# Finished rows of the experts scattered back to their tokens, the last layer's into the output

## The chip, the cores and the metric

The program runs on one core of a Trainium2 chip. The core has TensorE (PE, matmuls), VectorE (DVE), ScalarE (ACT), GpSimd (POOL) and SyncE (SP), and 16 DMA engines. The metric is the device time of one execution in microseconds; lower is better.

## The reference

Six sub-layers over 4 x 512 = 2048 tokens of 128 numbers: a ternary-weight feed-forward, a softmax attention with a second "moving" term, the same feed-forward, then a routed feed-forward, a linear attention, and the routed feed-forward again. The routed one is what the change is about:

```python
    def _L1_ffn_ref(x, Wr, W1, W2):                      # x is the normalised input
        probs = softmax(xf @ Wr); eidx = argmax(probs)   # E = 8 experts
        rank = number of earlier tokens with the same expert
        keep = rank < cap                                # cap = 2048 / 8 = 256
        xe = xf[dispatch]                                # [E, cap, 128]
        h = jnp.maximum(jnp.einsum('ecd,edf->ecf', xe, W1), 0.0)
        ye = jnp.einsum('ecf,efd->ecd', h, W2) * (pe * valid)[:, :, None]
        y = zeros.at[dispatch].add(ye)                   # dropped tokens get 0
    x = x + 0.5 * _L1_ffn_ref(_layernorm(x), ...)
    x = x + _L1_attn_ref(_layernorm(x), ...)
    x = x + 0.5 * _L1_ffn_ref(_layernorm(x), ...)
```

With the given inputs one or two experts get nearly all tokens: 556 tokens are kept in the first routed layer and 572 in the second; the other slots of the 8 x 256 stay empty.

## The kernel before

The order of every engine's work is written out by hand; engines wait on semaphores. The tokens stand in SBUF as four batches `x[b]`, each 128 partitions x 4 tiles x 128. A batch is normalised (DVE's `moments` and `normalise`, with the root between them on POOL, `rsqrt`), turned by TensorE, and so on.

A routed layer goes so. For each batch DVE works out (`place`, L1009) for each token a row number `slot_all` and a factor `gate_all` (0 for a dropped token); a dropped token has a spare row behind the 2048 real ones. POOL sends the four tiles of normalised rows to these rows of `xe_scr` in HBM (`scatter`, L569, four indirect DMAs of 128 rows). When all are there, SP loads each expert's 256 rows (`rows_in`, L494), and for each of eight experts TensorE turns them (L1677), multiplies by the first weights (`up`), ACT and DVE apply the relu to one half each (L870, L1214), TensorE multiplies by the second weights (`down`), DVE copies the result from PSUM (L1218), SP stores it to `ye_scr` (L500). TensorE does `up` of the next expert ahead of `down` of this one; results, hidden tiles and rows have 2, 2 and 4 buffers.

Then the answers come back by token. After the first routed layer POOL gathers for each batch four tiles of 128 rows of `ye_scr` by `slot_all` (`gather`, L577 to L587), and DVE's `combine` (L1220) adds gate times row to `x[b]` and goes on with the norm of the linear attention. The gathers of batches 1 to 3 stand in POOL's row between its other work of that attention. After the second routed layer POOL gathers all sixteen tiles (L720), DVE sums (L1371), SP stores `x[b]` to the output (L538).

The rows that a dropped token points to in `ye_scr`, and the rows of `xe_scr` that no token fills, are set to zero by four DMAs at the start (L344); DVE waits for them ahead of its fourth batch.

## Time and profile before

| | us |
|---|---|
| three runs | 706.55, 710.32, 709.92 (median 709.92) |
| the profiled execution | 705.89 |
| its span, first to last instruction | 704.1 |
| busy: PE / DVE / ACT / POOL | 506.5 / 365.7 / 196.7 / 181.9 |
| mean granted TensorE clock | 0.881 of full speed |

The first routed layer's expert stage lies at 415 to 453 us of the span, the linear attention's entries at 462 to 500, its loop to 622, the second expert stage at 639 to 676, the rest is the way back to the output. A chain of waits follows the work that ended last back through what released it; a timeline lists the instructions of an engine with the idle time ahead of each and what ended it.

### The profile page before, as it was taken

The numbers are of one execution on the slowest core, as the hardware profiler recorded it, in microseconds if no ns is written. First come the engines' busy times: TensorE is split into PE (matmuls) and PEld (weight loads), VectorE is DVE, ScalarE is ACT, GpSimd is POOL, SyncE is SP. The second block draws the span as 40 slices with busy tenths as digits, with TensorE's granted clock in tenths as the row PEclk, the third lists the DMA queues.
The fourth block names the chain that finished last, engine by engine and source line by source line (L and its number), as shares of the span: only waits on it lengthen the run. The fifth ranks groups of instructions, "written<-read, shape, count | busy, mean of one in ns | idle before, by whom it ended". The sixth has DMA issues, their size and how long they took to land.

```text
span 704.1 us, 9924 instructions
## 1 busy us (share of the span) xinstructions
PE 506.5 (72%) x3706; PEld 323.5 (46%) x3706; DVE 365.7 (52%) x950; ACT 196.7 (28%) x278; POOL 181.9 (26%) x208
## 2 busy tenths in 40 slices
PE   1777775998899999988686639634788888735930
PEld 1654322445444544533475528522454655424920
DVE  4555482668667676820655412135778777330221
ACT  1454313451543245065235002112123111101200
POOL 8564360000101010010023350044402022031035
PEclk9999896999999999999999559956999999656975
DMA  7537877332633422060430021107652620001213
GB/s 267 210 117 244 266 246 197 120 99 62 139 101 89 126 80 80 29 159 15 134 106 16 19 64 49 38 27 178 186 149 54 190 70 16 1 16 52 61 41 101
DMA packets 61471, 74.16 MB, mean 105 GB/s; under 512 B 6772, under 2 KB 38128, under 8 KB 61168
## 3 DMA queue, kind: packets, MB, share of 16 engines
q1 hardware_dynamic: 59376, 69.34, 33.6%
q0 software_dynamic: 2048, 4.20, 2.1%
q8 instruction: 29, 0.48, 0.3%
q14 instruction: 18, 0.15, 0.1%
HBM read 42.97 MB, written 30.41 MB: 104 GB/s over the span
## 4 chain that ended last, share of the span: by engine, by line
PE 46%; DVE 17%; POOL 8%; SPq 8%; issue 8%; DMA 7%; ACT 5%; POOLq 0%; DVEq 0%; ACTq 0%
PE ps_accum L1379 21%; PE ps_pair L1379 15%; PE ps_turn L1379 5%; POOL xe_scr L574 3%; DMA sb_ring<-sb_qs 3%; SPq L358 2%; DVE sb_work L1133 2%; PE ps_turn L1387 2%; POOL sb_work L720 2%; POOL sb_rstd L558 2%; DVE sb_work L1271 2%; DVE sb_mpart L1059 1%; SPq L352 1%; DVE sb_stats L960 1%; DVE sb_values L969 1%
## 5 line engine op out<-in xcount | busy, mean ns | idle before, releaser
L812 ACT ACTIVATE sb_work<-ps_pair 128x1024 f32<-128x1024 f32 x80 | 80.3, 1026 | 50.7 <-PE ps_pair L1379 49.8
L1379 PE MATMUL ps_pair<-sb_ring,sb_xsets 128*128 128x512 f32 x160 | 64.6, 480 | 11.4 <-DMA sb_ring<-sb_qs 5.7
L1059 DVE TENSOR_REDUCE sb_mpart<-ps_turn 128x4 f32<-128x512 f32 x80 | 55.0, 687 | 31.2 <-PE ps_turn L1379 31.1
L1059 DVE TENSOR_REDUCE sb_mpart<-ps_accum 128x4 f32<-128x512 f32 x80 | 55.0, 688 | 19.2 <-PE ps_accum L1379 18.2
L1379 PE MATMUL ps_accum<-sb_work,sb_v_aug 128*32 128x128 f32 (+3 forms) x768 | 57.7, 394 | 0.3 <-ACT sb_work L812 0.3
L1379 PE MATMUL ps_turn<-sb_ring,sb_m_sets 128*128 128x512 f32 x80 | 39.5, 494 | 10.0 <-DVE sb_mpart L1059 9.8
L1379 PE MATMUL ps_accum<-sb_ring,sb_m_sets 128*128 128x512 f32 x80 | 41.8, 523 | 4.5 <-DVE sb_mpart L1059 3.9
L1379 PEld LDWEIGHTS ps_pair<-sb_ring,sb_xsets 128*128 128x128 f32 x160 | 30.7, 199 | 22.5 <-issue 10.7
L624 POOL TENSOR_TENSOR sb_e_pad<-sb_v_next,sb_y_ar 128x128 f32<-128x128 f32 x16 | 7.3, 457 | 127.2 <-DVE sb_y_ar L1103 127.2
L1271 DVE TENSOR_TENSOR sb_work<-ps_pair,sb_cst 128x1024 f32<-128x1024 f32 x32 | 37.5, 1214 | 2.2 <-PE ps_pair L1379 2.2
L1133 DVE TENSOR_TENSOR sb_work<-ps_pair,sb_cst 128x1024 f32<-128x1024 f32 x32 | 37.7, 1218 | 0.9
L556 POOL TENSOR_SCALAR sb_ve<-sb_mv 128x4 f32<-128x4 f32 x24 | 5.6, 233 | 124.5 <-DVE sb_mv L963 124.3
L1379 PE MATMUL ps_pair<-sb_y_tmp,sb_mw 128*128 128x256 f32 x128 | 34.1, 414 | 1.9 <-ACT sb_y_tmp L862 1.9
L574 POOL DMA_INDIRECT xe_scr<-sb_values,sb_slot_all x16 | 15.9, 994 | 73.4 <-DVE sb_slot_all L1040 69.8
L1387 PE MATMUL ps_turn<-sb_cst,sb_values 128*128 128x128 f32 x48 | 10.3, 354 | 34.1 <-DVE sb_values L969 29.6
L1379 PE MATMUL ps_accum<-sb_mw,sb_work 128*128 128x128 f32 x256 | 31.3, 276 | 2.3 <-issue 2.3
L1379 PE MATMUL ps_pair<-sb_xs,sb_w1r 128*128 128x512 f32 x64 | 22.1, 470 | 15.0 <-DVE sb_xs L979 7.4
L1379 PEld LDWEIGHTS ps_accum<-sb_mw,sb_work 128*128 128x128 f32 x256 | 30.0, 192 | 2.8 <-issue 2.6
L1218 DVE COPY sb_e_pad<-ps_accum 128x256 f32<-128x256 f32 x16 | 6.8, 425 | 44.7 <-PE ps_accum L1379 44.7
L1379 PE MATMUL ps_pair<-sb_ring,sb_ka_stk 128*128 128x512 f32 x64 | 24.4, 492 | 7.6 <-DVE sb_work L1271 4.9
L734 ACT COPY sb_xnT<-ps_turn 128x512 f32<-128x512 f32 x16 | 9.3, 583 | 70.6 <-PE ps_turn L1387 70.6
L1379 PEld LDWEIGHTS ps_pair<-sb_y_tmp,sb_mw 128*128 128x128 f32 x128 | 25.4, 210 | 6.6 <-ACT sb_y_tmp L862 3.4
(242 smaller groups left out, 1002.2 us busy)
## 6 DMA issues: line engine op xcount, KB each, us to landing
sb_m_sets<-q_scr SPq DMA_DIRECT2D x16, 256.0 KB
sb_xsets<-k_scr SPq DMA_DIRECT2D x16, 256.0 KB
sb_ka_stk<-mk_scr SPq DMA_DIRECT2D x4, 1024.0 KB
sb_mw<-in_mw SPq DMA_DIRECT2D x16, 256.0 KB, 5.6
sb_ka_stk<-mk_scr SPq DMA_DIRECT2D x8, 512.0 KB
q_scr<-sb_qs SPq DMA_DIRECT2D x12, 256.0 KB, 3.1
k_scr<-sb_ks SPq DMA_DIRECT2D x12, 256.0 KB, 3.9
sb_ring<-k_scr SPq DMA_DIRECT2D x64, 48.0 KB
```

Source lines behind the costliest of these rows:

```text
L358: sp.dma_start(ring[VW * hl:VW * hl + 3 * HD, i, hl].bitcast(F32), head_rows(q_scr, b, HL * hs + hl, 3 * HD)).then_inc(done, 16)
L558: pool.tensor_tensor(rstd[i][:], ve[i][:], const("minus_half"), ALU.pow).then_inc(s["rstd"], 1)
L574: pool.indirect_dma_start(xe_scr, bass.IndirectOffsetOnAxis(ap=places[:, t:t + 1], axis=0), rows_out[:, t, :], None).then_inc(s["scattered ...
L624: pool.tensor_tensor(dst, value, answer, ALU.subtract).then_inc(s["err_pad"], 1)
L720: pool.indirect_dma_start(y_last[:, b, t, :], None, ye_scr, bass.IndirectOffsetOnAxis(ap=slot_all[:, i:i + 1], axis=0)).then_inc(last_gath ...
L734: act.copy(dst, bank[:]).then_inc(s["x2_ready"], 1)
L812: act.activation(banks[:, 2 * i:2 * i + 2], pair[u % 2][:], ACT.Exp, scale=SCALE).then_inc(s["exp_done"], 1)
L1059: dve.tensor_reduce(mpart[:, m // NPAIR, m % NPAIR, :], max_banks[m % 2][:].rearrange("p (h k) -> p h k", h=HL), AX.X, ALU.max).then_inc(s ...
L1133: dve.tensor_tensor(work[:, n % 4].rearrange("p a (h q) -> p (a h) q", h=HL), pair[n % 2][:].rearrange("p a (h q) -> p (a h) q", h=HL), bc ...
L1271: dve.tensor_tensor(work[:, n % 4].rearrange("p a (h q) -> p (a h) q", h=HL), pair[n % 2][:].rearrange("p a (h q) -> p (a h) q", h=HL), bc ...
L1379: return pe.matmul(dst, lhsT, rhs, start=start, stop=stop, skip_group_check=True)
L1387: last = pe.transpose(tile(dst, t), src[:, t, :], ident)
```

## The change

1. A row that goes out to the experts (`rows_out`) has 258 numbers: the 128 normalised ones, the token's number, its gate, and the 128 of the not normalised x (`RW = 2 * D + 2`; `ID, GATE, OLD = D, D + 1, D + 2`). DVE writes them at once in this layout; there is one more small DVE instruction in `place`. The two layers have an `xe_scr` each.
2. On evacuation DVE does 2 multiply-adds instead of a copy: result x gate + old x. So what leaves an expert is the finished row of its token.
3. POOL casts the row numbers of the loaded rows (`places_of`) and scatters each expert's two tiles straight to `y_scr` (first layer) or `out` (second) while the next experts run. Before, SP has stored every batch's old x there (`keep_old`), for the dropped tokens.
4. An empty slot carries a number from 2048 on. In the first layer these rows go behind the real ones of `y_scr`; for `out` the DMA has a bound on the row number, and skips them. To this end SP fills the first 2048 rows of each `xe_scr` (six DMAs of 128-column or 2-column runs) ahead of the experts' weights.
5. After the first layer SP loads `x[b]` from `y_scr`; `combine` is now `entry`, without the sums. After the second nothing is left but SP's wait. All gathers, the fills at the start, `gate_all` and the four stores of `x[b]` go.
6. The rows out of the first layer lie where `ring` is, so POOL sets that part to zero again ahead of `scatter_back(0)`; SP waits for it ahead of the linear attention's first stores. The experts' rows and the second layer's rows out share the place of `e_pad`.
7. A load of rows into one of the four buffers now waits for the evacuation of the expert that had it, too.

```diff
-            def gather(b): ...
+            def places_of(n):
+                pool.wait_ge(xg_loaded[n % 4], 16 * (n // 4 + 1))
+                if n >= 4:
+                    pool.wait_ge(ye_kept[n % 2], 16 * NG * ((n - 2) // 2))
+                pool.tensor_copy(places_back[:, n % 4, :], xg[:, n % 4, :, ID]).then_inc(s["places_in"], 1)
+            def scatter_back(m):
+                for kept in old_kept[m]:
+                    hold(pool, kept, 16 * B // (m + 1))
+                places_of(E * m)
+                for e in range(E):
+                    n = E * m + e
+                    if e + 1 < E:
+                        places_of(n + 1)
+                    pool.wait_ge(s["places_in"], n + 1)
+                    hold(pool, s["ye_evac"], n + 1)
+                    for g in range(NG):
+                        pool.indirect_dma_start(y_scr[m], bass.IndirectOffsetOnAxis(ap=places_back[:, n % 4, g:g + 1], axis=0),
+                                                ye[n % 2][:, g, :], None, bounds_check=(2 - m) * NTOK - 1,
+                                                oob_is_err=False).then_inc(ye_kept[n % 2], 16)
...
+            pool.wait_ge(s["scattered"], 16 * NT * B)
+            pool.wait_ge(old_kept[0][0], 16 * B)
+            pool.memset(ring[:, 0:2].bitcast(F32), 0.0).then_inc(s["zeroed"], 1)
+            pool.memset(ring[:, 2, 0, 0:B * NT * RW - 2 * HL * T].bitcast(F32), 0.0).then_inc(s["zeroed"], 1)
+            scatter_back(0)
...
+                dve.tensor_scalar(rows_out[r // B][b][:, :, ID], spare[:], float(-NTOK), None, ALU.add)
...
-                    dve.tensor_copy(ye[:, n % 2].rearrange("p g d -> p (g d)"), accum[n % 2][:, 0:NG * D]).then_inc(s["ye_evac"], 1)
+                    for g in range(NG):
+                        last = dve.scalar_tensor_tensor(out=ye[n % 2][:, g, :], in0=accum[n % 2][:, g * D:(g + 1) * D],
+                                                        scalar=xg[:, n % 4, g, GATE:GATE + 1], in1=xg[:, n % 4, g, OLD:RW],
+                                                        op0=ALU.mult, op1=ALU.add)
+                    last.then_inc(s["ye_evac"], 1)
...
+            for scr in xe_scr:
+                spill = scr[0:NTOK].rearrange("(p r) d -> p r d", p=P)
+                for c, src in ((0, bc(const("ident"), NTOK // P)), (OLD, bc(const("ident"), NTOK // P)),
+                               (ID, const("spill_ids").rearrange("p (r d) -> p r d", d=2))):
+                    sp.dma_start(spill[:, :, c:c + src.shape[2]], src).then_inc(s["spill_in"], 16)
...
+            for b in range(B):
+                sp.dma_start(x[b][:], tile_rows(y_scr[0], b)).then_inc(x_loaded[b], 16)
+            hold(sp, s["zeroed"], 18)
```

POOL's row from the last scatter of the second layer to its end, before (`sb_work` is where the answers by token landed):

```order
L558 TENSOR_TENSOR sb_rstd<-sb_ve,sb_cst 128x4 [waits s_var_eps]
L574 DMA xe_scr<-sb_values,sb_slot_all 4096x128 [waits s_rank_j,s_pad_zero]
L574 DMA xe_scr<-sb_values,sb_slot_all 4096x128 x3
L720 DMA sb_work<-ye_scr,sb_slot_all 128x128 [waits s_ye_mm,s_ye_kept1,s_ye_kept0]
L720 DMA sb_work<-ye_scr,sb_slot_all 128x128 x15
```

and of the change (`sb_expert_rows` the loaded rows, `sb_y_tmp` the finished ones, `sb_places_back` their row numbers):

```order
L566 TENSOR_TENSOR sb_rstd<-sb_ve,sb_cst 128x4 [waits s_var_eps]
L585 DMA xe_scr<-sb_exit_rows,sb_slot_all 4096x258 [waits s_rank_j]
L585 DMA xe_scr<-sb_exit_rows,sb_slot_all 4096x258 x3
L593 CAST sb_places_back<-sb_expert_rows 128x2 [waits s_kept1,s_kept2,s_ye_kept0,s_xg0]
L593 CAST sb_places_back<-sb_expert_rows 128x2 [waits s_ye_kept1,s_xg1]
L607 DMA out<-sb_y_tmp,sb_places_back 2048x128 [waits s_places_in,s_ye_evac]
L607 DMA out<-sb_y_tmp,sb_places_back 2048x128
L593 CAST sb_places_back<-sb_expert_rows 128x2 [waits s_ye_kept0,s_xg2]
...
L607 DMA out<-sb_y_tmp,sb_places_back 2048x128 [waits s_places_in,s_ye_evac]
L607 DMA out<-sb_y_tmp,sb_places_back 2048x128
```

The sixteen gathers behind the last evacuation are gone, and sixteen scatters stand in pairs, each behind its expert's evacuation (`s_ye_evac`). The same pairs stand in the first layer.

SP's row ahead of and behind the first expert stage, before (`sb_mw` the experts' weights):

```order
L400 DMA sb_ring<-sb_qs 1x4x512
L477 DMA sb_mw<-in_mw 128x512 [waits s_st_mm,s_ma_mm]
L478 DMA sb_mw<-in_mw 128x4x128
...
L494 DMA sb_e_pad<-xe_scr 128x2x128 [waits s_scattered]
L494 DMA sb_e_pad<-xe_scr 128x2x128 x3
L494 DMA sb_e_pad<-xe_scr 128x2x128 [waits s_xg_t]
L500 DMA ye_scr<-sb_e_pad 128x2x128 [waits s_ye_evac]
...
L500 DMA ye_scr<-sb_e_pad 128x2x128 [waits s_ye_evac] x5
L352 DMA mq_scr<-sb_qs 16x8x512 [waits s_l1_lo]
```

and of the change:

```order
L397 DMA sb_ring<-sb_qs 1x4x512
L476 DMA xe_scr<-sb_cst 2048x1x128 [waits s_st_mm]
L476 DMA xe_scr<-sb_cst 2048x1x128
L476 DMA xe_scr<-sb_cst 2048x1x2
...
L479 DMA sb_mw<-in_mw 128x512 [waits s_ma_mm]
...
L483 DMA y_scr<-sb_wide_rows 128x4x128 [waits s_ffn_x] x4
L504 DMA sb_expert_rows<-xe_scr 128x2x258 [waits s_scattered,s_kept0,s_spill_in]
L504 DMA sb_expert_rows<-xe_scr 128x2x258 x3
L504 DMA sb_expert_rows<-xe_scr 128x2x258 [waits s_ye_evac,s_places_in,s_xg_t] x4
L511 DMA sb_x<-y_scr 128x4x128 [waits s_ye_kept0,s_ye_kept1]
...
L349 DMA mq_scr<-sb_qs 16x8x512 [waits s_zeroed,s_l1_lo]
```

The fills stand ahead of the weights, the old x is stored ahead of the first rows' load, the stores of the answers are gone, and the four loads of x wait for both of POOL's semaphores.

## Rows read from the trace of the kernel before

**Rows 1.** The page: span, and the chain that ended last by line.

```profile
span 704.1 us, 9924 instructions
...
PE ps_accum L1379 21%; PE ps_pair L1379 15%; PE ps_turn L1379 5%; POOL xe_scr L574 3%; DMA sb_ring<-sb_qs 3%; SPq L358 2%; DVE sb_work L1133 2%; PE ps_turn L1387 2%; POOL sb_work L720 2%; POOL sb_rstd L558 2%; DVE sb_work L1271 2%; DVE sb_mpart L1059 1%; SPq L352 1%; DVE sb_stats L960 1%; DVE sb_values L969 1%
```

**Rows 2.** Chain of waits, 640 us to the end: start, us, what.

```profile
675.82 0.44 DVE sb_e_pad L1218
...
678.10 0.73 issue
...
697.62 2.36 DMA sb_work<-ye_scr,sb_slot_all
```

**Rows 3.** Chain of waits from 450 to 470 us.

```profile
452.60 0.44 DVE sb_e_pad L1218
...
463.17 0.89 DVE sb_stats L960 x4
```

**Rows 4.** Timeline 655 to 675 us: start, us, engine, line, operation, count, [idle before <-releaser].

```profile
658.26 0.68 DVE L1214 TENSOR_SCALAR sb_work<-ps_pair 128x512 f32<-128x512 f32 x1
...
659.67 1.95 PE L1379 MATMUL ps_accum<-sb_mw,sb_work 128*128 128x128 f32 x16
...
661.65 0.42 DVE L1218 COPY sb_e_pad<-ps_accum 128x256 f32<-128x256 f32 x1 [2.71 <-PE ps_accum L1379]
662.00 0.68 DVE L1214 TENSOR_SCALAR sb_work<-ps_pair 128x512 f32<-128x512 f32 x1
...
666.92 0.38 PE L1677 MATMUL ps_turn<-sb_cst,sb_e_pad 128*128 128x128 f32 x2
...
673.76 1.47 PE L1379 MATMUL ps_accum<-sb_mw,sb_work 128*128 128x128 f32 x11 [1.16 <-issue]
```

**Rows 5.** Timeline of POOL; last, the sixteen last gathers: ns min/median/max.

```profile
413.70 1.82 POOL L676 MEMSET sb_h_act<- 128x2048 f32 x1
...
588.07 1.09 POOL L574 DMA_INDIRECT xe_scr<-sb_values,sb_slot_all  x1 [20.55 <-DVE sb_slot_all L1040]
589.46 0.97 POOL L574 DMA_INDIRECT xe_scr<-sb_values,sb_slot_all  x1 [0.31 <-issue]
...
L720 POOL DMA_INDIRECT sb_work<-ye_scr,sb_slot_all x16: 940/944/999, 678.8 to 697.6; - x16
```

**Rows 6.** Chain of waits, start of the first expert stage.

```profile
412.56 2.22 DMA xe_scr<-sb_v_next,sb_slot_all
414.80 2.23 DMA sb_e_pad<-xe_scr
```

**Rows 7.** Timelines of SP and of DVE at the start.

```profile
0.73 0.45 SPq L318 DMA_DIRECT2D sb_x<-in_x  x1
...
3.65 0.87 DVE L960 BATCH_NORM_STATS2 sb_stats<-sb_x 128x6 f32<-128x128 f32 x4 [3.65 <-DMA sb_x<-in_x]
```

**Rows 8.** Timelines of DVE and TensorE, entries of the second attention.

```profile
466.17 1.32 DVE L969 TENSOR_SCALAR sb_values<-sb_x,sb_mv,sb_rstd 128x128 f32<-128x128 f32 x4 [1.60 <-POOL sb_rstd L558]
...
493.66 1.21 PE L1379 MATMUL ps_pair<-sb_ring,sb_ka_stk 128*128 128x512 f32 x4 [2.31 <-DMA sb_ka_stk<-mk_scr]
...
494.92 2.34 DVE L1271 TENSOR_TENSOR sb_work<-ps_pair,sb_cst 128x1024 f32<-128x1024 f32 x2
...
502.50 1.10 DVE L969 TENSOR_SCALAR sb_values<-sb_x,sb_mv,sb_rstd 128x128 f32<-128x128 f32 x4
...
526.63 1.13 DVE L1224 SCALAR_TENSOR_TENSOR sb_x<-sb_e_pad,sb_gate_all,sb_x 128x128 f32<-128x128 f32 x4
```

**Rows 9.** Timelines of SP and POOL; then stretches: us, TensorE busy, clock, DMA share, GB/s.

```profile
343.01 0.35 SPq L477 DMA_DIRECT2D sb_mw<-in_mw  x1
...
378.15 1.25 POOL L574 DMA_INDIRECT xe_scr<-sb_y_tmp,sb_slot_all  x1 [6.89 <-DVE sb_slot_all L1040]
...
416.00:420.00 4.00, 2.32 (x6) 0.50 0.53 159
608.00:644.00 36.00, 14.00 (x78) 0.50 0.11 33
```

More of the change, by code:

```diff
@@ L255, in build @@
         v_scr = dram("v_scr", [B, T, D])
-        xe_scr = dram("xe_scr", [2 * NTOK, D])
-        ye_scr = dram("ye_scr", [2 * NTOK, D])
+        xe_scr = [dram(f"xe_scr{m}", [2 * NTOK, RW]) for m in range(2)]
+        y_scr = [dram("y_scr", [2 * NTOK, D]), out]
         def tile_rows(ap, b):
@@ L534, in _ @@
                     load_l1(b + 1, 1)
-            experts(1)
-            for b in range(B):
-                sp.wait_ge(s["mixed"], NT * (B + b + 1))
-                sp.dma_start(tile_rows(out, b), x[b][:]).then_inc(s["out_done"], 16)
-            sp.wait_ge(s["out_done"], 16 * B)
-            for kept in ye_kept:
-                sp.wait_ge(kept, 16 * E)
-            sp.wait_ge(s["scattered"], 16 * NT * B * 2)
+                if b:
+                    hold(sp, s["l1_x"], b)
+                    keep_old(1, b - 1)
+            hold(sp, s["l1_x"], B)
+            keep_old(1, B - 1)
+            experts(1)
         @block.gpsimd
@@ L693, in _ @@
             rsqrt(norm_of_entry(1), 1)
-            gather(2)
             base(1)
@@ L950, in _ @@
             router_exp(2 * B - 1)
-            act.wait_ge(s["scattered"], 16 * NT * 2 * B)
+            for left in sent[1]:
+                act.wait_ge(left, 16 * NT * B // 2)
             relu_experts(1)
@@ L1676, in turn_rows @@
                     for g in range(NG):
-                        last = pe.transpose(tile(turn[n % 2], g), xg[:, n % 4, g, :], ident)
+                        last = pe.transpose(tile(turn[n % 2], g), xg[:, n % 4, g, 0:D], ident)
                     last.then_inc(s["xg_t"], 1)
```

166 lines of the change are left out of this document (74 added, 92 removed).

## The prediction

> **What bounds the kernel now.** I read the page first. The chain that ended last runs through TensorE's matmuls into its three kinds of PSUM tiles for 41% of the span (21, 15 and 5), so what matters is which handovers stand between its busy stretches [rows 1]. So I read the chain in order of time next, at the two places that the change touches: from the first expert stage into the second attention, and from the second expert stage to the end.
>
> At the end nothing but POOL works. The last expert result leaves PSUM at 675.82 + 0.44 = 676.26; then come the store of the answers, 0.73 us before POOL's first gather, sixteen gathers one behind the other of which the last starts at 697.62, its landing and the sum behind it [rows 2]. From 676.26 to the span's end at 704.1 that is 27.84 us. At the first stage's end it is the same pattern for one batch: last result at 452.60 + 0.44 = 453.04, DVE's statistics of batch 0 start at 463.17, so 10.13 us [rows 3].
>
> Inside an expert stage TensorE sets the pace: DVE's relu of one expert starts 662.00 - 658.26 = 3.74 us after that of the expert before, and TensorE starts on the relu's tile at 659.67, 0.73 us after the relu ended (658.26 + 0.68). Only the last expert is different: there TensorE waits 1.16 us for a relu that stands behind an evacuation [rows 4].
>
> **End of the second stage.** The sixteen gathers, the sixteen sums and the four stores of the output go. In their place POOL scatters each expert's two tiles when they are evacuated. Only the last expert's pair lies behind the end of TensorE's work. From evacuation to landing: 0.02 to wake, 0.75 before the first DMA (0.73 at 678.10), 1.39 from its start to the second's (588.07 to 589.46, first 1.09 and 0.30 of issue) [rows 2, 5], and 2.22 from a scatter's start to its landing [rows 6]: 4.38 us, say 4.5 with SP's last wait. 27.84 - 4.5 = 23.3 us gained.
>
> This holds if POOL keeps up. Per expert it now does 0.75 + 1.09 + 0.30 + 0.96 for the pair and about 0.3 for the cast of the row numbers and its wait (an estimate from the 0.30 between two POOL instructions): 3.4 us of 3.74 [rows 4, 5]. The bound on the row number is in no row. Per DMA I bound it at -0.2 (rows out of range are never moved) and +1.0 (each DMA twice as dear), and take 0, because gathers and scatters, different as they are, both cost 0.94 to 0.97 behind another one [rows 5].
>
> **First stage to attention.** POOL's gathers of batch 0 and their sum go; instead the rows are complete in HBM after the same 4.38 us, and SP loads x. The nearest row for that load is the kernel's first one, of the same 256 KB in 512-byte pieces: issued at 0.73, DVE starts on it at 3.65, so 2.92 us [rows 7]. 4.38 + 0.05 + 2.92 = 7.35 instead of 10.13: 2.8 us gained. Bounds: 2.2 for the load, as half the bytes take now (414.80, 2.23) [rows 6], and 4.5 if the four loads share the queues; so 1.2 to 3.5.
>
> **Entries of the second attention.** Each of the four sums (1.13 for four tiles [rows 8]) goes; that of batch 0 is counted above. Batch 0's and 1's normalising takes 1.32 where POOL's next instruction is a gather, batch 2's 1.10 where it isn't [rows 8], so 0.2 comes back at batch 0. At batch 1 DVE would be 1.1 + 0.2 sooner, but what is late next is the load of the stacked features: TensorE's first scores waited 2.31 us for it and started at 493.66, their first half (0.6 us) is ready at 494.3, and DVE's mask began at 494.92 [rows 8]. So only 0.6 of the 1.3. Batch 2 gives 1.1. Batch 3 stands in the attention loop where TensorE is nearly as late, and I take 0.8. Together 0.2 + 0.6 + 1.1 + 0.8 = 2.7 us, bounds 0.8 and 3.7.
>
> The Trainium skill (SBUF — State Buffer, section SBUF: two separate sides) says that VectorE and GpSimd hold a shared port pair one at a time, when VectorE is in a fast mode or reads two SBUF operands. The 1.32 beside 1.10 agrees with that. For the new scatters beside DVE it speaks against the change only if the evacuation were such an operation; it reads PSUM and one SBUF operand, so by the rule nothing is added, and if it were locked the last relu would be 0.2 us later per stage.
>
> **Starts of the expert stages.** A row that goes out now is 258 numbers, not 128. The last scatter's landing and the first load stand bare on the path: 2.22 and 2.23 us [rows 6]. For 66 KB more in the scatter I take 0.3 (bounds 0.1 and 0.45). The load grows from 128 to 258 KB; the 2.92 of a 256 KB load against 2.23 gives 0.7, the rate of [rows 9], 159 GB/s at a share of 0.53, so some 300 GB/s, gives 0.4; I take 0.6 (0.4 to 0.9). One more tiny DVE instruction for the row number stands before the slot's: 0.1. So 1.0 per stage, 2.0 in all, bounds 1.2 and 2.9.
>
> The Trainium skill (DMA: Bandwidth & Descriptors, section Anatomy of one DMA — SWDGE (gpsimd) path) puts a DMA at about 2.0 us fixed plus its bytes at 436 GB/s. The 2.22 for 64 KB agrees. By that page the wider rows would cost 0.15 and 0.3 and the two starts 1.1 together, and the time would be 0.9 us lower.
>
> **Inside the stages.** One copy of 256 columns (0.42, and the relu starts 0.35 behind it [rows 4]) becomes two multiply-adds of 128. The sums of now are four in 1.13, so some 0.26 apart and 0.35 the last: the relu starts 0.2 later, the evacuation ends 0.17 later. For experts 0 to 6 the 0.73 us hides it. For the last one both count: 0.37 per stage, 0.75 in all. If the cover were gone, it would be 0.2 for each expert, 3.2 us. Loads of rows for expert n now wait for the evacuation of n - 4; for expert 7 that is 661.65 + 0.42 and its turn comes at 666.92 [rows 4], so a load has 4.8 us, for some 2.9.
>
> **What is hidden.** SP's fill of the rows without a token (4 MB and two columns of 8-byte runs) is issued ahead of the weights, so at 343.01 at the latest, and is needed by the first scatter at 378.15: at least 35 us of cover [rows 9]. At 300 GB/s the 4 MB take 14 us. The 4096 short runs have no row; between 0.03 us for each on its queue, as a 512-byte piece takes at that rate, and four times that, they cost 7 to 31 us of 16 queues' time. The expert weights come behind it and are needed at 417, so they have 39 us more. POOL's new memset of 4096 columns is twice the 1.82 of [rows 5]; with as much again for the two beside it POOL is through at 413.70 + 1.82 + 1.82 + 3.64 = 421; the first expert result comes at 452.60 - 7 x 3.74 = 426.4. Storing the old x (four 256 KB stores per layer) stands between loads that wait for later events. The fills at the start that go are waited for by DVE ahead of batch 3, where it has work of its own: I take nothing, and at most 1 us gained.
>
> **Sum.** -23.3 - 2.8 - 2.7 + 2.0 + 0.75 = -26.0 us. The profiled execution took 705.89 with a span of 704.1; it becomes 679.9. The three runs are 706.55, 709.92 and 710.32, so their median of 709.92 lies 4.0 above the profiled one, and all four executions together have their middle at 708.2. I add half of the gap, 1.8, and forecast 681.5 us.
>
> **Rivals.**
> 1. POOL can't keep up. There is 0.3 us of slack per expert. If the bound costs 0.3 us per DMA, a pair takes 4.0 and seven experts lag 0.3 each in both stages: 2 x 2.1 and 0.3 for the last pair each time, about 5 us, 686.5. For it: the slack is thin and the bound unseen. Against it: POOL's time differs by 0.03 between a scatter and a gather [rows 5]. Chance 0.10.
> 2. The other side: POOL's time for a scatter goes by the row's bytes. 24 of the 32 scatters into the experts' rows stand on the path (3% of the span in [rows 1], 21 us, and the last of each layer), each 0.96 to 1.09, and the chain runs through them before POOL's root for the next norm [rows 5]. If a row of 258 numbers cost twice that of 128, that is 24 x 0.96 = 23 us: 704.5, a gain within the error. It turns slower than before from 1.1 us more per scatter on. For it: every indirect row in the trace has 128 numbers, so nothing excludes it. Against it: 0.96 for 128 rows of 512 bytes is far from being moved by POOL itself, since the landing comes 1.3 us after. Chance 0.06, half of it slower.
> 3. TensorE's granted clock falls elsewhere. It stood at 0.50 (1.2 GHz) from 608 to 644, with TensorE busy for 14.0 us of it [rows 9]; at 2.4 GHz that work would take 7 us less, of which some 4 stand on the path. With the stages shifted by 4 us the drop may come elsewhere, longer or not at all: 4 us either way, 677.5 or 685.5. Chance 0.15, together.
> 4. The short runs of the fill are so slow that the first scatter waits. 256 runs on each of 16 queues use the cover up from 0.08 us each ((35 - 14) / 256); at 0.15 they add 17 us, 698. Chance 0.03.
> The forecast has what is left, 0.66.
>
> **How the numbers follow.** A change of under 0.5%, 3.5 us, can't be told from none here. Forecast, rivals 1, 3 and 4 are all faster: 0.94. Rival 2 is split, 0.03 the same (with what is unforeseen) and 0.03 slower. The range: downwards the best bounds (1.0 for the gains, 0.8 for the starts), the clock's 4 and an execution like the profiled: 674. Upwards rival 1 with runs like the slowest: 691.
>
> **What would show it.** Right: POOL DMAs in pairs 3.7 us apart in both expert stages, 0.95 to 1.1 each; the span ends 4 to 5 us after DVE's last multiply-add; DVE's first statistics of the second attention 7 to 8 us after the first stage's last evacuation; the wide scatters still 0.96. Wrong: the pairs drift away from the evacuations (1), the scatters of 258 numbers take more (2), or POOL's first scatter waits on a DMA of the fill (4).

## The result and the profile after

Over the runs of one chip the kernel before took 708.23 us (median of four, 706.21 to 710.32) and the changed kernel 685.34 us (median of four, 682.54 to 687.47): ratio 0.9674, 95% interval 0.9623 to 0.9726, so **3.3% faster**. On a second chip, in five rounds, it was 687.50 against 709.12, ratio 0.9697 (0.9655 to 0.9739). The profiled execution took 686.09 with a span of 684.3, 19.8 us less than the profiled one of before. A median is over all executions of a run; executions more than 1.5% above the fastest of the same kernel are left out of the ratios.

The page of the changed kernel, span and chain by line; it answers to [rows 1]:

```profile
span 684.3 us, 10016 instructions
...
PE ps_accum L1395 23%; PE ps_pair L1395 17%; PE ps_turn L1395 5%; DMA sb_ring<-sb_qs 3%; POOL xe_scr L585 3%; SPq L355 2%; PE ps_turn L1403 2%; POOL sb_rstd L566 2%; DVE sb_work L1152 2%; DVE sb_mpart L1078 1%; DVE sb_work L1290 1%; SPq L349 1%; DVE sb_stats L975 1%; PE ps_turn L1825 1%; DMA sb_expert_rows<-xe_scr 1%
```

`POOL sb_work L720`, 2% of the chain before, is gone, and none of the lines listed is a scatter back (L607).

The end, timelines of DVE and POOL of the changed kernel (start, us, engine, line, operation, [idle before <-releaser]), and the last wait of SP (us in total, times, longest); it answers to [rows 2]:

```profile
675.02 0.61 DVE L1239 SCALAR_TENSOR_TENSOR sb_y_tmp<-ps_accum,sb_expert_rows 128x128 f32<-128x128 f32 x2 [2.16 <-PE ps_accum L1395]
...
676.49 0.97 POOL L607 DMA_INDIRECT out<-sb_y_tmp,sb_places_back  x1 [1.11 <-issue]
677.77 0.97 POOL L607 DMA_INDIRECT out<-sb_y_tmp,sb_places_back  x1 [0.30 <-issue]
...
SPq L116 <- PEq L116: 4.1, 1, 4.1
```

The last two scatters go out as forecast, 0.86 and 1.28 us apart. The last one's landing frees SP at 680.2, 4.5 us behind the last result, as forecast too. But the span ends at 684.3, 8.67 us after the last result: SP spends the last 4.1 us waiting for nothing but the other engines at the end of the program (L116).

The first stage's end, chain of waits of the changed kernel; it answers to [rows 3]:

```profile
453.97 0.34 DVE sb_y_tmp L1239
...
455.42 0.97 POOL y_scr L607
456.39 0.30 issue
456.69 2.24 DMA y_scr<-sb_y_tmp,sb_places_back
...
459.02 2.83 DMA sb_x<-y_scr
...
461.95 0.89 DVE sb_stats L975 x4
462.83 0.03 issue
462.86 0.02 DVEq L313
462.88 0.44 issue
463.32 0.39 DVE sb_mv L978 x4
```

From the last result (454.58) to the statistics 7.37 us, as forecast (7.35). Half a microsecond of issue stands behind the statistics, where the kernel before had 0.13 (463.17 + 0.89 to its aggregation at 464.19).

The starts of the expert stages, chain of the changed kernel; it answers to [rows 6]:

```profile
412.64 2.92 DMA xe_scr<-sb_wide_rows,sb_slot_all
...
415.73 2.69 DMA sb_expert_rows<-xe_scr
...
633.68 2.71 DMA xe_scr<-sb_exit_rows,sb_slot_all
...
636.61 2.67 DMA sb_expert_rows<-xe_scr
```

POOL's indirect DMAs, all of a line of the changed kernel: duration ns min/median/max, first and last start; they answer to [rows 5]:

```profile
L585 POOL DMA_INDIRECT xe_scr<-sb_wide_rows,sb_slot_all x16: 956/961/1248, 379.2 to 412.6; - x16
...
L607 POOL DMA_INDIRECT out<-sb_y_tmp,sb_places_back x16: 969/974/999, 651.0 to 677.8; - x16
```

At the median a scatter of 258 numbers takes POOL 0.96 us as one of 128 did, and a scatter back 0.97.

**Where the time went, by stretch.** Each row is the distance between two instructions of the traces: the last scatter of a layer, TensorE's first turn of expert rows, the end of DVE's last evacuation, the first entry turn. "Again" is a second profiled execution of the unaltered changed kernel (run after_again).

| stretch | before | changed | again | forecast of change |
|---|---|---|---|---|
| to the last scatter, layer 1 | 412.56 | 412.64 | 414.90 | 0 |
| to the first expert turn | 4.60 | 5.92 | 5.91 | +1.0 |
| first expert stage | 35.86 | 36.02 | 35.92 | +0.37 |
| to the first entry turn | 14.62 | 11.98 | 11.94 | -2.8 and -0.2 |
| attention, to the last scatter | 169.08 | 167.12 | 163.49 | -2.5 |
| to the first expert turn | 4.36 | 5.65 | 6.08 | +1.0 |
| second expert stage | 35.16 | 36.30 | 36.17 | +0.37 |
| to the end | 27.86 | 8.67 | 8.69 | -23.3 |

Two terms stand out: the end brought 19.2 instead of 23.3, and the attention brought 2.0 in one execution and 5.6 in the other. The experiments go to these first.

### The profile page after: what moved, and what is told of

Same layout as the page of the kernel before. It is cut to its first block, busy times and chain, and to the rows that moved or that the text cites. A ratio compares the mean times of both kernels' runs of the same rounds, so it can differ in the third digit from the quotient of the medians.

```text
span 684.3 us, 10016 instructions
## 1 busy us (share of the span) xinstructions
PE 509.8 (75%) x3706; PEld 326.6 (48%) x3706; DVE 358.7 (52%) x942; ACT 196.7 (29%) x278; POOL 189.0 (28%) x226
## 3 DMA queue, kind: packets, MB, share of 16 engines
q0 software_dynamic: 2560, 5.58, 2.3%
## 4 chain that ended last, share of the span: by engine, by line
PE 50%; DVE 17%; POOL 8%; issue 8%; ACT 6%; DMA 6%; SPq 5%; POOLq 0%; DVEq 0%; ACTq 0%
PE ps_accum L1395 23%; PE ps_pair L1395 17%; PE ps_turn L1395 5%; DMA sb_ring<-sb_qs 3%; POOL xe_scr L585 3%; SPq L355 2%; PE ps_turn L1403 2%; POOL sb_rstd L566 2%; DVE sb_work L1152 2%; DVE sb_mpart L1078 1%; DVE sb_work L1290 1%; SPq L349 1%; DVE sb_stats L975 1%; PE ps_turn L1825 1%; DMA sb_expert_rows<-xe_scr 1%
## 5 line engine op out<-in xcount | busy, mean ns | idle before, releaser
L1395 PE MATMUL ps_accum<-sb_work,sb_v_aug 128*32 128x128 f32 (+3 forms) x768 | 59.1, 402 | 0.3 <-ACT sb_work L826 0.3
L585 POOL DMA_INDIRECT xe_scr<-sb_exit_rows,sb_slot_all x16 | 15.9, 995 | 74.7 <-DVE sb_slot_all L1059 71.0
L1239 DVE SCALAR_TENSOR_TENSOR sb_y_tmp<-ps_accum,sb_expert_rows 128x128 f32<-128x128 f32 x32 | 9.8, 346 | 42.6 <-PE ps_accum L1395 42.6
L1395 PEld LDWEIGHTS ps_accum<-sb_work,sb_v_aug 128*32 128x32 f32 x768 | 17.6, 111 | 21.9 <-issue 13.8
```

The lines of the kernel that those rows point to most:

```text
L585: pool.indirect_dma_start(xe_scr[m], bass.IndirectOffsetOnAxis(ap=slot_all[:, i:i + 1], axis=0), rows_out[m][b][:, t, :], None).then_inc(s ...
L1239: last = dve.scalar_tensor_tensor(out=ye[n % 2][:, g, :], in0=accum[n % 2][:, g * D:(g + 1) * D], scalar=xg[:, n % 4, g, GATE:GATE + 1], i ...
L1395: return pe.matmul(dst, lhsT, rhs, start=start, stop=stop, skip_group_check=True)
```

## The experiments

Times are medians beside runs of the kernel before on the same chip; a ratio is to these. "Spans" and distances are from the one profiled execution of each run.

**What sets the end.** Run tail_two_less:

```diff
+                    if m == 1 and e >= E - 2:
+                        continue
                     for g in range(NG):
                         pool.indirect_dma_start(y_scr[m], ...)
```

> The changed kernel without the last four of the 32 indirect DMAs of the way back in the second stage: the rows of its last two experts never reach the output, nothing else is left out. In the changed kernel the span ended 8.6 us after the last result of the experts left VectorE (675.73 to 684.3) and 6.5 us after the start of GpSimd's last indirect DMA (677.77), though DMA traffic stopped at 680. Theory A, GpSimd takes some 6.5 us from the start of its last indirect DMA to the end of its program, and that sets the end: the last one now starts at about 671.2, so the span ends at 677.7, 2 us behind the last VectorE result, 6.6 us earlier (about 678.7 us on the median). Theory B, the end comes a fixed 4.3 us behind whatever comes last of landings and results: here the last result at 675.7, so the span ends at 680.0, 4.3 us earlier. Theory C, a fixed 8.6 us behind the last result whatever is sent: 684.3, no change.

Measured: 680.82 us, ratio 0.9603 (0.9558 to 0.9647), span 679.2. None of the three: POOL's last DMA starts at 669.49, DVE's last result ends at 673.93, the span 5.27 behind that. A look at the code tells why: the `continue` stands behind POOL's wait for the result, so POOL's program still ended with that wait, not with the DMA. Run tail_pool_early lets POOL's loop end two experts earlier, waits included (`mine = E - 2 * m`, `for e in range(mine)`):

> As tail_two_less (the rows of the last two experts of the second stage never reach the output), and GpSimd's waits for their results are gone too, so its program ends with the sixth expert's second indirect DMA. In tail_two_less GpSimd still waited for the last result (VectorE's end at 673.93) and the span ended 5.3 us behind that, 679.2; in the kernel before, the kernel before with one store, the first half alone and the changed kernel it ended 5.5 to 5.6 us behind GpSimd's last indirect DMA, while VectorE's last instruction stood only 2.7 to 2.9 us ahead of the end in the first three. Theory A', GpSimd's program takes 5.3 to 5.5 us to end behind its last instruction or wait, the other engines 2.7 us at most: the span now ends at most 2.7 us behind VectorE's last result and not before 5.5 us behind GpSimd's last DMA, some 2.5 us earlier than in tail_two_less (about 676.6, 678.4 us with what lies around it). Theory B', 5.3 us behind the last result whoever waits for it: no change against tail_two_less, 679.2.

Measured: 678.95 us, ratio 0.9588 (0.9521 to 0.9654), span 675.2. Timelines of POOL and DVE of this run:

```profile
669.01 0.97 POOL L608 DMA_INDIRECT out<-sb_y_tmp,sb_places_back  x1 [0.30 <-issue]
...
673.15 0.61 DVE L1240 SCALAR_TENSOR_TENSOR sb_y_tmp<-ps_accum,sb_expert_rows 128x128 f32<-128x128 f32 x2 [2.16 <-PE ps_accum L1396]
```

The end now stands 1.44 us behind DVE's last result (673.76), and 5.22 behind POOL's last DMA (669.98). Theory B' wanted 679.2. (The last result itself came 0.2 us earlier in this trace than in the other, so of the 4.0 us between the spans 3.8 are the end's.) The two runs of this pair were on different chips, so their medians don't tell them apart; the distances inside the traces do.

Run before_one_store (the kernel before; `if b == 0:` ahead of the last stores):

> The kernel before with the stores of batches 1 to 3 of the output left out (their rows are not written); the gathers and VectorE's mixing stay. Its last indirect DMA started at 697.62, its last mixing ended at 701.24, the last store was issued at 701.27 and the span ended at 704.1. Theory A (GpSimd's end, 6.5 us behind the start of its last indirect DMA): the end stays at 704.1, no change within 0.3 us, and the stores of the kernel before cost nothing at its end. Theory B (a landing and a fixed tail behind it): without the last store's landing the span ends some 1.8 us earlier, 702.3, the time by 1.8 us less.

Measured: 709.37 us, ratio 1.0010 (0.9968 to 1.0051), span 705.2. Timelines of POOL and DVE:

```profile
698.68 0.94 POOL L721 DMA_INDIRECT sb_work<-ye_scr,sb_slot_all  x1 [0.30 <-issue]
...
701.38 1.14 DVE L1372 SCALAR_TENSOR_TENSOR sb_x<-sb_work,sb_gate_all,sb_x 128x128 f32<-128x128 f32 x4 [4.08 <-DMA sb_work<-ye_scr,sb_slot_all]
```

From the end of POOL's last DMA (699.62) to the span's end 5.58 us, with the last store gone; with it, in the kernel before, 5.54 (698.56 to 704.1). So in the kernel before too the sums and stores of the last batch were hidden behind POOL's way out, and my 27.84 us had them as its last terms. In the changed kernel the same distance is 5.56 (678.74 to 684.3). Theory A stands, with a number put right: the span ends 5.2 to 5.6 us behind POOL's last DMA or wait, where the first expectation had 6.5 from the start of the last DMA, and VectorE needs 1.44 at most. What POOL does in that time no row shows, nor why it is 5.22 and 5.27 in the two shortened kernels and 5.50 or more elsewhere.

**The two halves.** Run first_half_only puts the way back of the second stage as the kernel before has it (SP's stores, the sixteen gathers, the sums, the stores of the output), with rows of 128 numbers there:

```diff
-            scatter_back(1)
+            for b in range(B):
+                for t in range(NT):
+                    pool.indirect_dma_start(y_last[:, b, t, :], None, ye_scr, ...)
```

> The change in the first expert stage alone; the second stage sends 512-byte rows, stores results in order, gathers them and mixes and stores the output, as the kernel before does. By the two traces the changed kernel stood 3.04 us ahead of the kernel before at the last scatter of the second stage, which is all that the first half gives. Theory A (the two halves add): 3.0 us faster than before, 705.2 us against 708.2, ratio 0.996 (TensorE's clock in the attention between the two, which took about 2.1 us twice in the changed kernel, may add or take 4 us). Rival: the first half gives nothing or costs by itself, since attention waits for something else (spill fill, later expert weights), and the whole gain of the change is the second half's: 0 to +1 us.

Measured: 701.70 us, ratio 0.9890 (0.9858 to 0.9922), span 699.4. The interval of the gain is 0.8 to 1.4%, 5.5 to 10 us, and the trace says 4.7. So the first half gives more than the 3.0 of theory A. In its trace the attention takes 163.58 us from the first entry turn to the last scatter, as in "again" (163.49) and unlike the 167.12 of the first trace. The spans also hold the first 412 us, where nothing was altered and which differ by some us between traces. From the last scatter of the first stage to the end it is 291.5 us before, 284.7 with the first half and 268.2 in "again": the first half gives 6.8 and the second 16.5, and they add up to the 23.3 of the whole.

**The attention and the clock.** Windows of the changed kernel: us, then busy time (instructions) of PE, PEld, DVE, ACT and POOL, granted clock, DMA share, GB/s:

```profile
516.00:524.00 8.00, 7.72 (x56) 4.89 (x56) 3.61 (x7) 0.58 (x1) 0.00 (x0) 0.50 0.74 193
548.00:552.00 4.00, 4.00 (x36) 2.18 (x32) 1.27 (x2) 0.00 (x0) 0.00 (x0) 0.50 0.84 209
```

The same stretches of the kernel before:

```profile
516.00:524.00 8.00, 5.11 (x51) 3.72 (x49) 5.46 (x10) 0.86 (x2) 0.00 (x0) 1.00 0.68 209
548.00:552.00 4.00, 2.58 (x13) 2.29 (x13) 2.78 (x12) 0.71 (x2) 0.00 (x0) 0.71 0.36 101
```

In both kernels TensorE had idled 2.9 us just ahead of the first place, and of these two executions only that of the changed kernel fell to the lower level (0.50, 1.2 GHz) behind it: its 40 matmuls of a tile's answers took 4.99 us against 2.95. Run fill_the_gap:

```diff
+                    pe.wait_ge(s["l1_masked"], n - 1)
+                    for k in range((6, 3)[b]):
+                        mm(pair[n % 2][:, 0, 0:3 * D], ident, l1w[:])
                     pe.wait_ge(s["l1_yn"], NT * b + 3)
                     turn_key_features(b + 2)
```

> The changed kernel with nine matmuls more (fp32, 128x128 by 128x384, into a PSUM bank that is free then and is overwritten afterwards) in two waits of TensorE in the second attention: 6 at about 511.7, 3 at about 542.8, ahead of the turn of the key features. Theory A, the granted clock of 0.50 at 516 to 524 and 548 to 552 follows from TensorE's idle stretch ahead of it, and it is what held 40 matmuls into ps_accum at 4.99 and 5.20 us instead of about 3: with the waits filled the clock stays at 1.00 there, the two groups take 3.0 us, and the span shrinks by up to 4.2 us (some 2 to 4, to 681 to 684 on the median). Rival: the clock falls there all the same, or the time comes back behind the next wait for VectorE: no change within 0.5 us, or slower by up to 1 us where the filler outlasts the wait.

Measured: 686.28 us, ratio 0.9673 (0.9608 to 0.9738). Its windows:

```profile
516.00:524.00 8.00, 7.51 (x69) 4.99 (x68) 4.29 (x8) 1.17 (x2) 0.00 (x0) 1.00 0.73 184
548.00:552.00 4.00, 4.00 (x64) 2.39 (x62) 2.36 (x2) 0.39 (x3) 0.00 (x0) 1.00 0.89 247
```

The clock stands at 1.00 (2.4 GHz) in both places with the idle stretches ahead filled. That the fillers held it there this run does not show, since the clock of the two places changes from execution to execution with the waits as they were. Behind the same 2.9 us of idle the 8 us at the first place have 0.80 to 0.82 in four unfilled traces (after_again, first_half_only, tail_two_less, tail_pool_early), 1.00 in two (narrow_rows, one_piece_fill), and 0.79 in before_one_store against the 1.00 of the kernel before; at the second place all six have 1.00. What decides these runs don't show.

The time did not fall. Six fillers took 4.04 us in a wait of 2.9. At a later turn the filled kernel (594.41) stands 179.3 us behind its last scatter of the first stage, the unaltered one of after_again (594.32) 179.4, so up to there nothing is won or lost; then its clock stays low, and its last scatter of the second stage comes 3.2 us later (220.5 and 217.3 us behind the first stage's). The 8 us from that turn on, filled and unaltered:

```profile
594.40:602.40 8.00, 7.29 (x52) 4.78 (x50) 2.61 (x4) 1.17 (x2) 0.00 (x0) 0.50 0.00 0
```

```profile
594.30:602.30 8.00, 6.11 (x65) 4.37 (x64) 4.27 (x12) 1.40 (x3) 0.00 (x0) 0.86 0.01 2
```

Whether the unaltered kernel falls into the slow pattern of its first trace by itself was asked with after_again:

> The changed kernel once more, unaltered, beside the kernel before on this chip, so that its spread and its usual clock are known. In its first profiled run the stretch from the last result of the first expert stage to the last scatter of the second took 179.1 us (454.58 to 633.68), in the six other runs that have the same first half and an unfilled or nearly unfilled attention 175.3 to 175.7, and in one with two filled waits 178.8; the kernel before took 183.7 and 183.5. Theory A: 179.1 was the clock's luck (its matmul groups at 516 and 548 at half clock), and this run has about 175.5; ratio to the kernel before 0.965 to 0.970 over five rounds. Rival: the changed kernel falls into the slow pattern by itself and shows 178 to 179 again, ratio 0.970 to 0.975.

Measured: 687.50 us, ratio 0.9697 (0.9655 to 0.9739). From the first stage's last result to the second's last scatter 175.43 us (456.73 to 632.16), where the first trace had 179.10 and the kernel before 183.70 and 183.50 (before_one_store). Five more traces with this first half and unfilled waits lie at 175.3 to 175.7 (no_bound, whose clock was low there, apart). So the usual gain there is 8.2 us, 5.5 was forecast, and the first trace shows 4.6, as it lost 3.7 to the clock. The place of the loss bears this out: counted from the last scatter of the first stage, the first trace is 0.2 us later than after_again at the turn of the key features ahead of the first place (514.62 and 516.71), 1.4 at the one ahead of the second (545.71 and 546.61) and 4.0 behind it (553.98 and 552.26), and then no more; in between lie the two groups at 0.50. The ratio lies in the interval of the first.

**The clock held up, with and without the change.** Run keep_warm puts such matmuls (`warm(i, k)`: k matmuls into `pair[i]`) into all of TensorE's long waits from the first expert stage on:

> The changed kernel with matmuls that nobody reads (fp32, 128x128 by 128x384, about 0.67 us each at a granted clock of 1.00) in TensorE's long waits: 9 and 15 ahead of the first rows of the two expert stages, 15 and 8 ahead of the first two entry turns, 4 and 2 where the run with the filled gap had 6 and 3, 8 ahead of the last exit turn. The changed kernel's granted clock was 0.50 to 0.56 at 460 to 472, 480 to 492, 516 to 524 and 548 to 552 and about 0.5 at 416 to 420, and every matmul there took up to twice as long. Theory A, TensorE's own idle stretches bring the clock down (the filled gaps kept it at 1.00 from 508 to 560): with the waits filled it stays near 1.00 through these stretches; by the busy TensorE time at half clock on the path (3.3 at 418 to 426, 2.4, 3, 2.1, 2.1 and some 3 at 639 to 645) 8 to 14 us less, 671 to 677. Rival: the waits are needed by VectorE and DMAs anyway, or the fillers outlast the waits at half clock (1.33 us each) and push the path: within 2 us of the changed kernel, or slower.

Measured: 682.01 us, ratio 0.9636 (0.9564 to 0.9708), short of the 671 to 677 of theory A. From the last scatter of the first stage to the end 261.8 us against 271.7 and 268.2. Part of the fillers ended before the waits did, so two runs followed, warm_more and the same fillers in the kernel before:

```diff
+                warm(0, (12, 15)[m])
                 turn_rows(0)
...
+                warm(0, (18, 9)[b])
                 turn_entry(b)
...
+                    warm(0, 4)
                     scores(0, 0)
```

> As keep_warm with more of the idle matmuls: 12 and 15 ahead of the expert stages, 18 and 9 ahead of the first two entry turns, 4 ahead of the first scores, 4 and 2, and 8 ahead of the last exit turn. In keep_warm the first expert stage still began at half clock (4.0 us of idle behind its filler) and so did the scores at 496 (3.4 us of idle). From the last scatter of the first stage to the end keep_warm took 261.8 us against 265 to 271.7 of unfilled runs. Theory A: 2 to 4 us less than that, 258 to 260, and a median of 676 to 681. Rival: the fillers reach past the waits and the time stays at keep_warm's 682 or above.

> The kernel before with the same idle matmuls in the same waits as warm_more, so that the change is compared at a clock that both keep up. Theory A, the filler's gain and the change's gain add: some 8 us off the kernel before, 700 to 703, and the ratio of warm_more to it is the change's own, 0.966 to 0.970. Rival: the kernel before gains little by the filler (within 3 us), since the gathers and the mixing of the entries, which the change takes away, bound its attention at any clock.

Measured: warm_more 678.87 us, ratio **0.9562** (0.9514 to 0.9609), apart from the 0.9697 (0.9655 to 0.9739) of the unaltered changed kernel on the same chip: the fastest version here, 1.4% below the change alone. before_warm 706.26, ratio 0.9926 (0.9887 to 0.9965). The median of warm_more is in the 676 to 681 that its theory A wanted; that of before_warm is above the 700 to 703 of its theory A, and 2.9 us below the kernel before, which is within the 3 us of the rival. The change with both kernels filled is 0.9562 / 0.9926 = 0.963 (0.957 to 0.970, an estimate from the two intervals), the same as without fillers within the intervals. Windows of warm_more, then of after_again:

```profile
460.00:472.00 12.00, 11.67 (x47) 7.73 (x48) 2.00 (x11) 0.00 (x0) 3.89 (x4) 1.00 0.34 103
640.00:644.00 4.00, 3.54 (x18) 2.84 (x18) 0.69 (x1) 0.87 (x2) 0.00 (x0) 1.00 0.08 29
```

```profile
460.00:472.00 12.00, 2.66 (x6) 1.55 (x7) 2.37 (x12) 0.59 (x1) 2.54 (x3) 0.50 0.32 94
640.00:644.00 4.00, 3.73 (x10) 2.50 (x9) 0.59 (x1) 0.23 (x1) 0.00 (x0) 0.50 0.07 23
```

The work of these windows stands 7 us later in warm_more, since the first 412 us, where nothing was altered, differ between traces (last scatter at 421.89, and at 414.90 in after_again). At the same distance from that scatter as 460 to 472 of after_again is 467 to 479 of warm_more; from 469.25 to 481.25 it still has 1.00, where 462.26 to 474.26 of after_again has 0.53.

From the last scatter of the first stage to the end warm_more takes 258.9 us, before_warm 283.75 (412.85 to 696.6): 24.8 apart. The filler's gain is then 9.3 us of 268.2 in the changed kernel and 7.8 of 291.5 in the one before. The medians say 8.6 and 2.9. The second trace is not a usual one: its execution took 698.42, the second fastest of twelve (697.27 to 712.33), with the highest mean clock (0.922, the others 0.885 to 0.917), and four of the twelve are left out of the ratio. The ratio, 0.9926, says 5.3 us, and its interval 2.5 to 8.0. So the filler is worth less in the kernel before, or as much; these runs don't decide.

**Starts.** Run narrow_rows (`xe_scr` of 130 columns; rows sent and loaded without the old one, `in1=xg[:, n % 4, g, 0:D]`):

> The changed kernel with rows of 130 numbers (520 bytes) instead of 258 (1032 bytes) on the way to the experts in both stages: the old row is left out, the experts' finished row adds the normalised row in its place, and the fill of the spill rows has no old part. In the changed kernel the first TensorE turn of a stage came 6.0 us behind the start of the last scatter in both stages, 1.3 to 1.4 us later than in the kernel before: landing of the last scatter 2.92 and 2.71 us against 2.22 and 2.23, loads of the first expert's rows 2.69 and 2.67 against 2.23, the rest SP's further waits. Theory A, row width: both come back to 2.2 to 2.3 us, 1.1 us per stage, and the time falls by some 2.3 us (to 683.0 on the median); GpSimd's 0.97 us per indirect DMA stays. Theory B, it is the form (512-byte pieces against one row of 520, the further waits, other traffic at that place): the landing and the load stay within 0.2 us of the changed kernel's, no change.

Measured: 684.25 us, ratio 0.9652 (0.9601 to 0.9702). Chain of this run:

```profile
411.94 2.63 DMA xe_scr<-sb_wide_rows,sb_slot_all
...
414.76 2.24 DMA sb_expert_rows<-xe_scr
...
628.77 2.35 DMA xe_scr<-sb_exit_rows,sb_slot_all
...
631.35 2.31 DMA sb_expert_rows<-xe_scr
```

Last scatter to first turn is 5.20 and 4.93 us, against 5.92 and 5.65 of the changed kernel: the width costs 0.72 per stage, 0.45 and 0.36 of it at the load and 0.29 and 0.36 at the landing. One execution does not fix these sizes. In ten traces with 258 numbers the first start takes 5.61 to 6.10 us and in nine the second 5.65 to 6.08, so the width costs 0.4 to 0.9 and 0.7 to 1.15; their loads take 2.62 to 2.89 and their landings 2.67 to 3.08, so at the landing of the first stage (2.63) the width is not clear of the spread. Of the first stage's 1.3 the other 0.6 are SP's further waits (0.15) and a landing that stays longer than 2.22 with 520 bytes too. In first_half_only, whose second stage has rows of 128 numbers and the waits of the kernel before, that start is back at 4.49 us. The gain of two 0.7 is under what the medians can tell.

**The fill.** Run one_piece_fill:

```diff
-                for c, src in ((0, bc(const("ident"), ...)), (OLD, ...), (ID, const("spill_ids")...)):
-                    sp.dma_start(spill[:, :, c:c + src.shape[2]], src).then_inc(s["spill_in"], 16)
+                sp.dma_start(spill, bc(const("spill_row"), NTOK // P)).then_inc(s["spill_in"], 16)
```

> The changed kernel with the fill of the spill rows as one piece of 1032 bytes per row (two DMAs in all instead of six; the third of every three had 8-byte pieces), every filled row with the same row number, one past the last token, and the bound at the last token in both stages, so that the first stage's filled rows are left unwritten too. In the changed kernel the six DMAs were issued at 332.91 and SP was held by them for 20.02 us; the experts' weights followed at 353.04 instead of 343.01, and nothing waited. Theory A, the fill is hidden behind the last attention of the first layer either way: SP is held for a third of that or less, the first scatter, the last scatter of the first stage and the end stay where they are, no change within 0.3 us apart from the clock's luck. Theory B, the 8-byte pieces slow what runs beside them (the first scatter stood 1.07 us later than before): 1 to 2 us faster.

Measured: 687.73 us, ratio 0.9720 (0.9657 to 0.9782). Timelines of SP, the changed kernel and this run:

```profile
332.91 20.02 SPq L476 DMA_DIRECT2D xe_scr<-sb_cst  x6
```

```profile
334.18 2.79 SPq L474 DMA_DIRECT2D xe_scr<-sb_cst  x2
346.65 0.37 SPq L477 DMA_DIRECT2D sb_mw<-in_mw  x1
```

SP is held for 2.79 us instead of 20.02, the first layer's first and last scatter into the experts' rows stand 32.77 apart (380.48 to 413.25), in seven other traces of the changed kernel's kind 32.7 to 32.8 (and 32.63, 33.42 and 33.88 in warm_more, the first trace and keep_warm), and the first scatter is where theirs are (379.2 to 382.3 in the traces without many fillers). Nothing is won that these can tell: hidden, as forecast. The run changes the number of DMAs (two instead of six) together with the length of the pieces, so it doesn't say which of the two held SP.

**The bound.** Run no_bound (`y_scr` of the second stage a scratch of 4096 rows, `bounds_check` gone in both):

> The changed kernel with the second stage's rows written to a scratch of 4096 rows without a bound on the row number, as the first stage's bound never cuts (the output is not written). Every indirect DMA of the second stage then writes its 128 rows, where the bound lets through 556 or so of 2048 in all. Theory A, the bound costs GpSimd nothing and the rows that it drops save nothing that is waited for: 0.97 us per DMA and 0.30 between them stay, the end stays 5.5 us behind the last one, no change within 0.3 us. Theory B, the bound has a price on GpSimd (a check per index): its DMAs get shorter by 0.1 us or more, and the end comes as much earlier. Theory C, the dropped rows save time at landing and for the buffers: the writes land 0.3 to 1 us later, with no or little effect on the end.

Measured: 686.06 us, ratio 0.9649 (0.9601 to 0.9697). Its profiled execution had a lower clock from 568 us on, so only POOL's rows are read from it:

```profile
L607 POOL DMA_INDIRECT y_scr<-sb_y_tmp,sb_places_back x32: 956/962/994, 431.3 to 685.1; - x32
```

0.962 against 0.974 us: the bound costs POOL 0.012 us per DMA. In the first stage, where it never cuts, a scatter back of the changed kernel took 0.977 on the mean, in the second 0.975, so it costs that whether it cuts or not. The span ends 5.5 us behind the last one (686.08 to 691.6), as everywhere.

## Why the prediction was right, and where its sizes were off

The direction and the mechanism held, and the time (681.5 forecast, 685.34 measured, inside 674 to 691). By the spans of the two profiled executions the sum of -26.0 stands against -19.8, of which the clock took 3.7 back; by the medians (708.23 and 685.34) against -22.9, and by after_again, from the last scatter of the first stage on, against -23.3. That the time came within 4 us is in part luck: the end was forecast 4.1 us too good, the entries 2.9 too poor. (In the sum itself half of 4.0 is 2.0, not 1.8, and 679.9 + 1.8 is 681.7; nothing hangs on it.) Term by term:

- **End of the second stage**, -23.3 forecast, -19.2 measured. The step "from evacuation to landing, say 4.5 with SP's last wait" is the mis-sized one: the sequence in it was right (0.86, 1.28, 0.97), but the end hangs on POOL leaving its program, 5.56 us behind its last DMA, and not on the landing, which came in the 4.5. 0.86 + 1.28 + 0.97 + 5.56 = 8.67. I had subtracted landing, sum and store from the end of the kernel before as if they were its path; they were hidden behind the same 5.5 us.
- **First stage to attention**, -2.8 forecast. Result to statistics went from 10.13 to 7.37, -2.76. Of this 0.36 was lost again in the wait behind the statistics.
- **Entries**, -2.7 forecast, about -5.6 usual, -2.0 in the first trace with the clock's 3.7 against it. The cap at batch 1 was wrong. I took the load of the stacked features as fixed. It moved with the rest: SP issued its last piece 0.9 us earlier (485.26 against 486.20), and TensorE got it 5.98 us after that instead of 7.46 (491.24, and 493.66 of [rows 8]). POOL's gathers of batch 2 ran beside it in the kernel before, but they are not what made the 7.46: in before_one_store, with the same gathers beside it, it took 6.02, and without gathers 4.0 to 5.98 in the traces of the changed kernel's kind. So the cap was read off one slow load. Batch 1 gave 1.6, not 0.6, by the distance between the first two entry turns (16.46 to 14.83), and batch 2 1.2. The other 2.8 of the 5.6 lie behind the third entry turn: 1.5 from it to TensorE's next turn of answers, 1.3 from there on, where batch 3's sum went. The 1.5 were in no term of the sum, and they are chance at least by half: in the trace of before TensorE stood 1.40 us there ([1.40 <-issue], nothing named that it waited for) and the distance was 6.33, in before_one_store it was 5.60 without such a stop, in after_again 4.87.
- **Starts**, +1.0 each forecast, +1.3 each measured (1.0 to 1.5 and 1.3 to 1.7 over the traces with 258 numbers), the width 0.7 of it. The load of the second stage took 2.06 us before, not the 2.23 of the first.
- **Inside**, +0.37 each forecast. The first stage took 0.16 more, the second 1.1. In the second TensorE was 0.6 behind by the second expert's up matmuls (5.95 us against 5.34 from the first turn), at the lower clock level: its first eight up matmuls took 3.78 us against 3.47.
- **Hidden** costs were hidden: fill, memset (POOL waited 8.4 us for the first result of the experts after it), old rows, the bound.

The rivals: **1**, POOL can't keep up, is false: pairs start 3.2 to 4.0 us apart and POOL idles 0.8 to 1.6 ahead of each. **2**, time by row bytes, is false: 0.961 us for 258 numbers, 0.95 to 0.96 for 130 in narrow_rows. **4** is false: SP was held for 20.02 us of at least 35, and the first scatter stands where it does without the short pieces. **3**, the clock elsewhere, happened in the direction of the slower side: 3.7 us in the profiled execution, within the 4 allowed.

By the rule of the Trainium skill (DMA: Bandwidth & Descriptors, Anatomy of one DMA — SWDGE (gpsimd) path), 2.0 us and the bytes at 436 GB/s, the wider rows should have cost 0.15 at the landing (an estimate from that page's rate). The trace shows 0.5 to 0.7, of which narrow_rows gives 0.3 to 0.4 to the width. In the second stage (2.35 us against 2.67 at the least) the measurement decides against the rule; in the first (2.63 against 2.68 to 3.07) it doesn't settle it. What the Trainium skill (SBUF — State Buffer, SBUF: two separate sides) says of the shared port pair agrees with the trace: the normalising of batch 0 took 1.12 instead of 1.32 once no gather stood beside it.

## What to carry to other kernels

Before taking a tail off, ask which engine leaves the program last: a stretch that seems to end in a landing may have ended in GpSimd's exit all along, and it stays when the landing goes. A load that something "waits for" is a cap only if its own start stays as it is and it takes as long in another execution. When a change moves TensorE's waits, compare windows of granted clock over several executions before reading a gain or loss into the rest. Idle matmuls in TensorE's long waits are worth a try: in all of them they made the changed kernel 1.4% faster, in two of them nothing.

## What the runs showed of the hardware that was not expected

- The span ended 5.50 to 5.59 us behind GpSimd's last indirect DMA in twelve traces, gathers and scatters alike, and 5.22 and 5.27 behind its last DMA or wait in the two that cut its work short; VectorE needed 1.44 us at most.
- An indirect scatter costs GpSimd 0.96 us at the median for rows of 128, 130 and 258 numbers, and a bound on the row number 0.012 us more.
- Six fill DMAs, four with pieces of 512 bytes and two of 8, held SP for 20.02 us; the same rows in two DMAs with pieces of 1032 bytes 2.79 us.
- Two executions of one kernel differed by 3.7 us in 175, all of it in two places where the granted clock was 0.50 in one of them. With idle matmuls in TensorE's waits the clock was 1.00 at 460 to 472 and at 640 to 644, where it had been 0.50, 0.927 on the mean of the execution instead of 0.889, and the kernel 1.4% faster.
- The same load of 512 KB took 7.46 us from SP's issue to TensorE's start in the profiled execution of the kernel before and 6.02 in that of before_one_store, with the same gathers beside it.
